# Two-layer transformer kernel on one Trainium2 core: reordered work at the end of the attention values, earlier weight splits, tables loaded ahead

## What is computed

```python
h = layernorm(x) * (1 + ca) + sa
x = x + ga * attention(h)
h = layernorm(x) * (1 + cb) + sb
x = x + gb * ffn(h)
```

```python
scores = where(mask, q @ k.T * scale, NEG)
attn = softmax(scores)
out = (attn @ v) @ Wo.T + bo
...
y = sum_over_chosen(combine * (silu(x @ W1.T) * (x @ W3.T)) @ W2.T) + shared
```

## Time and profile before

| what | us |
|---|---|
| median of 3 runs | 672.17 |
| lowest, highest | 668.56, 675.68 |
| the profiled execution's own time | 665.51 |
| span of its instructions | 663.7 |
| mean granted TensorE clock in it | 0.984 of full |

### The profile page before, as it was taken

The page is one execution under the profiler, slowest core; times in us unless marked ns, Lnnn a source line. Parts: engine busy times, 40 slices in busy tenths (PEclk is TensorE's granted clock), DMA queues, the critical chain, the costliest instruction groups (busy, mean ns, idle before and its releaser), DMA issues.

```text
span 663.7 us, 10873 instructions
## 1 busy us (share of the span) xinstructions
PE 606.6 (91%) x3897; PEld 471.5 (71%) x3907; DVE 379.0 (57%) x757; ACT 302.3 (46%) x462; POOL 129.3 (19%) x137
## 2 busy tenths in 40 slices
PE   3898899798999999999998897889997999999995
PEld 3777645487788888888886565543445878888884
DVE  6477535966244444544457699792358543345455
ACT  3657275554233333333333473427864643333331
POOL 4501015323122222222230000000112331222220
PEclk9999899999899999999999899898999999999999
DMA  8364454100001111111100024301210001111101
GB/s 324 98 223 173 145 162 153 50 1 25 24 26 48 47 47 47 47 47 47 47 25 0 1 69 133 121 5 62 81 56 25 1 25 47 48 47 47 43 7 63
DMA packets 22194, 44.64 MB, mean 67 GB/s; under 512 B 3632, under 2 KB 7632, under 8 KB 22160
## 3 DMA queue, kind: packets, MB, share of 16 engines
q1 hardware_dynamic: 21840, 44.05, 20.8%
q10 hardware_dynamic: 320, 0.13, 0.1%
HBM read 33.16 MB, written 11.01 MB: 67 GB/s over the span
## 4 chain that ended last, share of the span: by engine, by line
PE 67%; DVE 19%; ACT 4%; issue 4%; DMA 2%; POOL 2%; SPq 0%; DVEq 0%; ACTq 0%; POOLq 0%
PE PS L557 32%; PE PS L980 16%; DVE nmx L1531 5%; PE PS L857 3%; PE PS L827 2%; PE PS L701 2%; PE PS L703 2%; DVE x L1601 1%; PE PS L601 1%; DMA w_raw<-in_wqkv 1%; PE PS L714 1%; DVE stats L1430 1%; DVE xn L1743 1%; ACT q_masked L1129 1%; PE PS L872 1%
## 5 line engine op out<-in xcount | busy, mean ns | idle before, releaser
L1273 ACT ACTIVATE qk_hi<-xn 128x512 fp32r<-128x512 f32 x82 | 51.7, 631 | 171.0 <-DVE xn L1743 139.6
L557 PE MATMUL PS<-h_hi,wqkv_hi 128*128 128x512 f32 x304 | 102.7, 395 | 1.9 <-DVE h_lo L1464 1.3
L557 PE MATMUL PS<-h_hi,wqkv_lo 128*128 128x512 f32 x272 | 92.8, 396 | 2.6 <-DVE xn L1653 2.6
L1740 DVE TENSOR_TENSOR prs<-prs,PS 128x512 f32<-128x512 f32 x60 | 41.2, 687 | 86.8 <-PE PS L557 78.3
L1747 DVE TENSOR_TENSOR qk_lo<-xn,qk_hi 128x512 fp32r<-128x512 f32 x70 | 48.4, 692 | 47.8 <-ACT qk_hi L1273 47.8
L1269 ACT ACTIVATE prs<-PS 128x512 f32<-128x512 f32 x82 | 48.7, 594 | 48.5 <-PE PS L557 48.5
L557 PEld LDWEIGHTS PS<-h_hi,wqkv_hi 128*128 128x128 f32 x304 | 57.2, 188 | 14.0 <-DVE h_lo L1464 1.7
L557 PE MATMUL PS<-h_lo,wqkv_hi 128*128 128x512 f32 x160 | 62.9, 393 | 0.0
L557 PEld LDWEIGHTS PS<-h_hi,wqkv_lo 128*128 128x128 f32 x272 | 51.1, 188 | 14.9 <-DVE xn L1653 4.3
L1531 DVE TENSOR_REDUCE nmx<-PS 128x512 f32 (+4 forms) x96 | 54.2, 637 | 4.4 <-PE PS L719 4.3
L980 PE MATMUL PS<-wqkv_hi,qk_hi 128*128 128x256 f32 x288 | 53.5, 285 | 0.9 <-POOL qk_lo L529 0.7
(11 more groups left out here) (251 smaller groups left out, 1223.4 us busy)
## 6 DMA issues: line engine op xcount, KB each, us to landing
fw_raw<-in_ffn SPq DMA_DIRECT2D x41, 384.0 KB, 3.1
qk_slot<-rows_scr SPq DMA_DIRECT2D x32, 200.0 KB
rows_scr<-qk_hi SPq DMA_DIRECT2D x16, 256.0 KB
qk_slot<-q_scr SPq DMA_DIRECT2D x32, 100.0 KB
rows_scr<-qk_lo SPq DMA_DIRECT2D x8, 256.0 KB
wmod<-in_wmod SPq DMA_DIRECT2D x1, 1536.0 KB, 14.3
x<-in_x SPq DMA_DIRECT2D x2, 512.0 KB, 4.0
wmod<-in_wmod SPq DMA_DIRECT2D x1, 1024.0 KB, 10.8
```

The lines of the kernel that those rows point to most:

```text
L557: ins = nc.tensor.matmul(dst, left(a, c), right(b, c), start=n == 0, stop=n == total - 1)
L1273: nc.scalar.activation(hidR[b][0], hid[b], ACT.Copy).then_inc(f["hi"], 1)
L1740: tt(hid[buf] if half is None else gu[buf], gact[buf], PS[:, 5, :], ALU.mult).then_inc(f["gu"], 1)
```

## The change

- SyncE: the loads of tiles 2 and 3 stand behind u = 17 and u = 21 instead of 21 and 26, with the same waits.
- GpSimd: values are copied two groups at a time (0 and 1 at the start; in each odd group g the groups g+1 and g+2); the splits of tiles 0, 1, 2 stand first in groups 2, 3, 4.
- TensorE: the wait for `gate_taken` in layer 0 moves from before unit 2 to before `values(0)`; the last of four chunks of the output projection is done after `early_up(0)`.
- ScalarE: an Exp activation on one element before the last `max_high` of each layer; `gates(0)` after exponential 1; tile 2 is split after unit 4n+1; a Silu activation on one element at the end of the exponentials.
- VectorE: normalise, outputs 5, outputs 6, h_low, outputs 7, early product 0, then the gate-and-adds.

```diff
@@ load_attention (SyncE)
-                        if u in (H + 5, H + 10):
-                            s = (u - H) // 10
+                        if u in (H + 1, H + 5):
+                            s = (u - H) // 4
                             load_ffn(l, 1, s, 2 + s)
@@ attention (GpSimd)
                     take_values(0)
+                    take_values(1)
                 for g in range(QUADS):
-                    if l == 0 and g + 1 < QUADS:
-                        take_values(g + 1)
+                    if g in (2, 3, 4):
+                        weights_low(l, g - 2, g % 2)
+                    for k in (g + 1, g + 2):
+                        if l == 0 and g % 2 and k < QUADS:
+                            take_values(k)
                     if g % 2:
                         out_low(l, g // 2)
-                    if g in (2, 3, QUADS - 2):
-                        i = min(g - 2, 2)
-                        weights_low(l, i, i % 2)
@@ values (TensorE)
                     if l == 0:
+                        if g == 0:
+                            pe.wait_ge(gate_taken, 2)
                         pe.wait_ge(a["vs"], SLOTS * (g + 1))
@@ values_pass (TensorE)
-                if l == 0:
-                    pe.wait_ge(gate_taken, 2)
@@ out_projection (TensorE)
                 project_out(l, 1, range(OC - 1), False)
+
+            def out_projection_rest(l):
                 pe.wait_ge(at[l]["ol"], CHUNKS)
                 project_out(l, 1, range(OC - 1, OC), False)
@@ ffn (TensorE)
                 early_up(0)
+                out_projection_rest(l)
                 early_up(1)
@@ ScalarE, both layers
+            def exp_table():
+                nc.scalar.activation(table_in[:, :], ct[:, 0, 0, 0:1], ACT.Exp)
...
+            exp_table()
             max_high(0, 1)
@@ attention (ScalarE)
                 if l == 0:
-                    gates(0)
                     act.wait_ge(split, 3)
...
-                    if u in (2 * n - 1, 3 * n - 1, 7 * n - 2):
-                        i = u // n - 1 if u < 4 * n else 2
+                    if l == 0 and u == 1:
+                        gates(0)
+                    if u in (2 * n - 1, 3 * n - 1, 4 * n + 1):
+                        i = (u + 1) // n - 2
                         weights_high(l, i // 2, i % 2)
+                nc.scalar.activation(table_in[:, :], ct[:, 0, 0, 0:1], ACT.Silu)
@@ attention_outputs (VectorE)
                 norm_scales(n, slice(0, 1))
+                normalise(n)
                 outputs(l, BQ + 1)
-                normalise(n)
                 outputs(l, BQ + 2)
+                h_low(n, 0)
                 outputs(l, BQ + 3)
-                h_low(n, 0)
+                early_product(l, 0)
                 dve.wait_ge(y_ps, 4 * l + 3)
                 first = gate_and_add(l, 0, 1, 0, Y1_BANK)
                 dve.wait_ge(y_ps, 4 * l + 4)
                 last = gate_and_add(l, 0, 1, 1, Y1_BANK + 1)
                 first()
                 last()
-                early_product(l, 0)
```

## The result

| | before | after |
|---|---|---|
| median us | 672.40 | 676.86 |
| lowest, highest | 665.36, 685.28 | 672.69, 687.41 |
| runs | 20 | 20 |

The ratio after / before is 1.0079, 95% interval 1.0056 to 1.0103: the changed kernel is slower by 5.3 us (0.0079 x 672.4). The forecast was 675.2, slower by 3.0, with a range of 668.0 to 681.0. Some executions of any of these kernels are disturbed, that is some per cent longer at a lower mean clock; ratios, intervals and mean clocks of runs are of the others, but the profiled execution of after (683.0 us) is a disturbed one, with TensorE at half clock from 457 to 485 us, so nothing behind 457 us is compared in it.

The account below looks back on a forecast made before the run. TensorE, with 67% of the chain that ended last, was taken as the bound. The terms -0.8 + 4.3 + 0.5 - 0.4 - 1.9 + 0.4 + 0.9 gave +3.0 us on the median 672.17: 675.2 us, range 668.0 to 681.0.

Parts of the forecast that it names:

- Part 2, unit 18: Layer 0: keys of unit 18 queue behind the load waiting for the first split; TensorE idles +4.3 us, bounds +3.0 and +4.8.
- Part 2, unit 22: Layer 0: load of tile 3 stands before the keys of unit 22, landing about 110.9; +0.5 us, bounds 0 and +1.5.
- Part 1: Layer 0 start: Exp table load hidden in ScalarE's idle time, gates behind exponential 1; -0.8 us, bounds -0.4 and -1.3.
- Part 3: Value copies two ahead and splits: copies are ready when TensorE asks; worth 0 by itself.
- Part 4: End of layer 0's values: normalise first, early_up(0) in the gap, batch 1 transposed earlier; -1.9 us, bounds -0.9 and -2.9.
- Part 5: End of layer 1's values: normalise adds +1.5 us before values 6; stage ends +0.4 us later, bounds -0.7 and +1.3.
- The clock: TensorE's clock may fall behind the idle 4.3 us; bounded by 0 and +1.7 us, half taken: +0.9.
- Rival (b): Clock falls fully there and again around 496 us, layer 1's keys late too: +7.0 us, 679.2 us; chance 0.18.

Follow-up runs that it names:

- experiment 2: Three kernels: changed kernel with only SyncE's two loads put back, 0.9949; kernel before with only load, split and copy moves, 1.0172; changed kernel without those moves, 0.9949.
- experiment 1: Changed kernel with 20 filler matmuls on TensorE ahead of unit 18 of layer 0; ratio 0.9994 to the kernel before, median 671.61 us.
- experiment 5: Kernel before with only the Exp activation, gates behind exponential 1 and TensorE's moved wait; four runs, median 669.14 us, no ratio.
- experiments 2 and 3: Changed kernel with loads and splits in their old places: value copies also as before, 0.9949 to the kernel before; copies kept two ahead, 0.9894.
- Experiment 6: experiment 4 with the output projection whole again before the first feed-forward unit in both layers; ratio 1.0128 to the kernel before, median 680.07 us.
- experiment 4: Changed kernel with GpSimd's first two splits moved into group 1, ahead of its first output chunk; ratio 0.9871 to the kernel before, median 662.42 us.
- experiment 2's second kernel: Kernel before with only the moves of weight loads, splits and value copies; ratio 1.0172 to the kernel before, median 683.39 us.
- experiment 2's third kernel: Changed kernel with weight loads, value copies and splits all as before; ratio 0.9949 to the kernel before, median 666.47 us.
- experiments 1 and 6: Filler kernels: 20 matmuls before unit 18 in the changed kernel, 0.9994; 20 before the last chunk in both layers of the whole-projection kernel, 1.0079.

## Why the prediction was right in direction and short in size

- **Part 2, unit 18.** Right in mechanism and time. The split ended at 99.79 (forecast 100.1), the keys released TensorE at 105.82 (105.34), and the wait was 4.94 us (4.3, at the bound of 4.8), since part 1 had won a little more. The three kernels of experiment 2 put it on the position of the two loads.
- **Part 2, unit 22.** +0.5 was forecast, 0 came: the keys had landed by 110.69, and at half clock TensorE reached it only at 113.66. In experiment 1, at full clock and with keys that came 1.5 us later behind the first load, the wait is there, 1.33 us, inside the bounds of 0 and +1.5.
- **Part 1.** -1.04 us, -0.8 forecast, shown alone by experiment 5. The table load was hidden as argued. The Trainium skill (ScalarE: Activation LUTs, What ACT_TABLE_LOAD costs) counts a drain beside the load, by which -2.2 was to be won; the trace of after disagrees too, with the next activation 0.01 us behind the load (129.59 + 1.28, 130.88).
- **Part 3.** "Worth 0 by itself" failed as a statement on the copies. I checked the copies against the end of the values before them, and not against what stands ahead of them in GpSimd's queue once VectorE's order is changed. By experiments 2 and 3 it is 2.24 us of wait, and a fall of the clock in the trace with it: the copies two ahead are what let part 4 move VectorE's outputs without a charge. In the sum nothing is off by it, as both stand in the change.
- **Part 4.** -2.1 us, -1.9 forecast. The contended normalise is gone: its longest instruction takes 414 ns, 1904 before, now that GpSimd is idle beside it. The Trainium skill's rule of a shared pair of ports (SBUF — State Buffer, SBUF: two separate sides) agrees with that. TensorE has `early_up(0)` in the gap. Experiment 6 shows the price without it.
- **Part 5.** The wait before values 6 was 1.96 us (0.66 + 1.5 = 2.2 forecast), but the stage ended 0.2 us earlier (27.03 against 27.25), not 0.4 later. The last projection waited only 1.0 us.
- **The clock.** The mis-sized term. The forecast took half of 1.7 us, with all of 1.7 as the upper bound, from a fall that lasted 4 us. Behind this wait the lower level lasted from 105.8 to 112.6 us at 0.50, 2.85 us of loss, and fillers alone brought the time back by 0.85%. Rival (b) had the fall in full and in its place, but priced it at 1.7 too.
- **The range.** Its upper end was put at 681.0 for rival (b) with unit 22 at its bound; by its own terms that is 679.2 + 1.0 = 680.2. The result is inside either.

The terms as the traces have them: 3.93 us to unit 18 (which holds -1.04 of part 1) + 2.45 to unit 22 - 2.1 - 0.2 = +4.1 us, of +5.3 measured (interval 3.8 to 6.9). The sum stands inside the interval. The forecast's +3.0 came nearer to this than its clock term deserved: +0.5 for unit 22 and +0.4 for layer 1 did not come, and that made up for part of what the clock cost more. Whether the 1.2 us between +4.1 and +5.3 are further falls of the clock or noise isn't shown.

## What to carry to other kernels

A DMA that waits for a semaphore holds every later one on its queue, so a load may be moved up only past those that nobody needs before the wait ends; here the two positions differ by 1.3%, and moving the work that ends the wait (experiment 4, 0.9871) is worth at least as much as moving the load back (0.9949; the intervals overlap). An idle stretch of the bounding engine is priced with what its clock does afterwards, and needed work in the gap is the cheap cure. A table is fetched ahead where its engine is idle, as Exp was here (1.0 us won, together with the later gates), not where work is already due behind it, as with Silu (0.5 to 0.6 us lost).

## What the runs showed of the hardware

- TensorE's idle stretches of 4.9, 6.7, 4.5 and 4.3 us (after, experiment 2's second kernel, experiment 6 in both layers) were each followed by a lower clock, and so was one of 2.24 us (experiment 2's third kernel); the one of 2.64 us before wasn't. So the length of the idle stretch doesn't decide it alone. In the first and the third the granted clock went to 0.50 over 6.8 us and 0.58 over 4. Filler matmuls in the gaps of 4.9, 4.5 and 4.3 us kept it at 1.00 (experiments 1 and 6).
- The clock also fell with TensorE busy all along, which no wait explains: the 10.20 us of experiment 1, the 16.00 us of experiment 2's second kernel, and in after:

```profile
184.00:191.00 7.00, 7.00 (x26) 6.13 (x27) 0.24 (x2) 0.78 (x2) 0.00 (x0) 0.53 0.00 1
457.00:485.00 28.00, 27.89 (x150) 9.12 (x148) 4.14 (x10) 15.26 (x19) 3.93 (x3) 0.51 0.10 30
```

- The mean granted clock of the runs was 0.961 to 0.976 for after (median 0.966), and 0.966 to 0.984 for the kernel before (medians 0.974, 0.977 and 0.975 on three chips). Whether one idle stretch weighs on later stages is open: experiment 1, which took away that stretch alone, brought 5.7 us against the 2.85 us seen beside it, but its interval takes in both.
- The keys behind the load of 384 KB landed 4.82 us after their issue (4.42 before). The same transfers in the same order made TensorE wait 0.40 us before and 4.94 us after: what differs is which keys they carry, and so when TensorE wants them.
